# 64 experts: gating a unit ahead of weighing, slot rows eight units ahead, matrices reloaded at the second product

## The chip, the cores and the metric

The kernel runs on one core of a Trainium2 chip. The metric is the time of one execution on the device in microseconds (us), lower is better. A core has engines with their own instruction queues: TensorE (PE, its weight loads PEld), VectorE (DVE), ScalarE (ACT), GpSimd (POOL) and SyncE (SP, which here only issues DMA transfers). They wait for each other through semaphores: an instruction raises one when it is done, another queue waits for a count.

## The reference

The program is a stack of four macaron layers on 4096 tokens of width 128, each with two half-weighted feed-forward parts around an attention part. The first layer's feed-forward, used twice, is the mixture with 64 experts. Cut to what matters:

```python
def _L0_ffn_ref(hidden_states, wg, shared_w1, shared_w2, expert_w1, expert_w2):
    gates = jax.nn.softmax(logits, axis=-1)
    w_topk, idx_topk = jax.lax.top_k(gates, TOPK)          # 8 of 64
    ...
    valid = rank < CAPACITY                                # 160 slots an expert
    buf = jnp.zeros((NUM_EXPERTS, CAPACITY, H), x.dtype).at[se, rank].set(x[st], mode='drop')
    h = jnp.einsum('ech,efh->ecf', buf, expert_w1)         # 128 -> 2 x 384
    x1, x2 = jnp.split(h, 2, axis=-1)
    out = jnp.einsum('ecf,ehf->ech', x1 * jax.nn.silu(x2), expert_w2)   # 384 -> 128
    y = out[se, jnp.clip(rank, 0, CAPACITY - 1)]
    y = jnp.where(valid[:, None], y * sw[:, None].astype(y.dtype), 0.0)
    combined = jnp.zeros((T, H), x.dtype).at[st].add(y)
    return (shared_out + combined).reshape(B, S, H)
```

## The kernel before

All is float32. The mixture is done in three steps. The routing computes gates and scatters each chosen token's normalized row into the slot rows, a table in HBM of 10240 slots (64 x 160); a slot's row holds the 128 values, 64 weights and the token's number. Then `experts` works through the slots. Then `combine` adds two tables of results to the tokens.

`experts` takes 64 units, one expert each, a unit being 160 slots as 2 blocks (A = 2) of 80. For unit n, in the names of the profile (`l0f1e_` in the first run, `l0f2e_` in the second):

- SP loads the slot rows into `row` and the expert's matrices into `m_w` (393 KB and 197 KB). `Matrices` has four places; the first four experts' are loaded during the routing.
- TensorE turns the rows (`turn`, L3040, into bank `x`), ScalarE copies them to `xeT` (`copy`, L3081).
- TensorE makes the first product (`hidden`, L3050, bank `h`), six matrices, shown as twelve in the profile.
- ScalarE takes the silu of one half (`bend`, L3087, `sT`), VectorE multiplies it with the other (the gating, L3109, `gT`).
- TensorE makes the second product (`output`, L3060, bank `o`).
- VectorE reads the token numbers (L3117, `idx`) and multiplies the result with the slot's weight (the weighing, L3119, `y`).
- GpSimd scatters `y` with addition into one of two tables, one indirect DMA for each of the two blocks (L3153); unit n goes to table n % 2.

The order is written out by hand, one loop for each engine. TensorE's step n is `hidden(n + 1)`, `turn(n + 2)`, `output(n)`. ScalarE's is `bend(n)`, `copy(n + 2)`. VectorE's is gating n, index n, weighing n. Buffers: `row` 4, matrices 4, `y` and `idx` 4 (a ring), all others 2. The waits between them: VectorE may write `idx` and `y` of unit n when both scatters of unit n - 4 have landed; GpSimd starts the scatters of unit n when those of unit n - 2, into the same table, have landed; SP waits for the weighing of unit n - 4 (`y_ready`) and then issues matrices and slot rows of unit n in this order.

In the first run VectorE has work of another layer beside this: `kernel.products`, one instruction behind each weighing, 31 of 128x1024 elements and then a few small ones (L1841 in the profile, tiles `l0f1e_big`); it reads two SBUF operands. All 64 units are written out on VectorE there. In the second run it has none, and VectorE runs `stream`: the first steps written out, then a loop, then the last steps. The other engines do so in both runs, with four units a round.

## Time and profile before

| | us |
|---|---|
| median of 3 runs | 3244.47 (3237.09 to 3246.55) |
| the profiled execution | 3241.42 |
| its span | 3239.7 |
| GpSimd busy in the span | 1782.6 (55%) |
| TensorE busy | 2516.1 (78%) |
| VectorE busy | 2043.3 (63%) |
| mean granted TensorE clock | 0.893 |

All rows below are of that one profiled execution. A duration in the timeline is that of one instruction, or of so many merged (x12); what stands in brackets is the time that its engine stood idle before it and what ended that. A wait is put down to whatever came last by the profile; "issue" means that nothing the profile shows ended it. Idle time of an engine that isn't the bottleneck costs nothing. The expert step of the first run lies near 207 to 457 us, that of the second near 761 to 998 us.

### The profile page before, as it was taken

The page shows a single profiled execution, that of the slowest core. Times are in us where ns is not written, and L with a number is a line of the kernel's source. Part 1 is how long each engine was busy: PE and PEld are TensorE (multiplying, and loading weights), DVE is VectorE, ACT ScalarE, POOL GpSimd, SP SyncE. Part 2 cuts the span into 40 slices and gives each one's busy share as a digit, 9 for nine tenths or more (in the row PEclk, how much of TensorE's full clock was granted, in tenths as well). Part 3 has the DMA queues.
Part 4 walks back from the last instruction along what each step waited for, and adds up shares of the span by engine and source line. Part 5 has one row for each costly group of instructions (what it writes and reads, how often), then busy time and mean ns, then how long its engine had stood idle before and what let it go on. Part 6 is the DMA issues. An engine that isn't in the chain of part 4 may idle for free. (4 is left out here: it accounts for less than half of the span.)

```text
span 3239.7 us, 68607 instructions
## 1 busy us (share of the span) xinstructions
PE 2516.1 (78%) x24634; PEld 1640.8 (51%) x24634; DVE 2043.3 (63%) x5869; ACT 1372.1 (42%) x2937; POOL 1782.6 (55%) x2004
## 2 busy tenths in 40 slices
PE   3478957778994658899988999582898986999682
PEld 2358844547882434655555555370333333555371
DVE  6845335772334635588845887325999998788513
ACT  2212213321221324366652666334776762666433
POOL 4737752663874212399942134573888885123564
PEclk8689977879997879899987999795999998999796
DMA  9228862224996434001001011222121210111133
GB/s 374 94 67 206 220 163 50 89 64 105 233 224 185 117 111 191 19 17 21 13 2 22 20 28 36 69 72 99 73 103 55 82 76 14 20 26 33 47 96 96
DMA packets 220035, 294.11 MB, mean 91 GB/s; under 512 B 34016, under 2 KB 176895, under 8 KB 213600
## 3 DMA queue, kind: packets, MB, share of 16 engines
q1 hardware_dynamic: 173280, 249.85, 24.7%
q0 software_dynamic: 44352, 39.40, 6.4%
q8 instruction: 174, 2.85, 0.4%
q10 hardware_dynamic: 2112, 1.05, 0.2%
q14 instruction: 117, 0.96, 0.1%
HBM read 181.88 MB, written 100.40 MB: 87 GB/s over the span
## 5 line engine op out<-in xcount | busy, mean ns | idle before, releaser
L3873 POOL TENSOR_TENSOR l3am_db<-l3am_du,l3am_bs 128x1024 f32<-128x1024 f32 x127 | 297.8, 2367 | 38.4 <-DVE l3am_hh L4111 34.6
L4111 DVE TENSOR_TENSOR_SCAN l3am_hh<-l3am_dA,l3am_db 128x1024 f32<-128x1024 f32 x128 | 292.3, 2285 | 0.9 <-ACT l3am_dA L4011 0.7
L1217 POOL TENSOR_TENSOR l2a_pT<-l2a_pT,kept 128x512 int32<-128x512 int32 x213 | 265.0, 1281 | 45.4 <-ACT l2a_pT L1423 45.4
L4242 PE MATMUL l3am_y<-l3am_hc,ident 128*128 128x512 f32 x512 | 242.3, 596 | 0.0
L3153 POOL DMA_INDIRECT l0f_table<-l0f1e_y,l0f1e_idx x128 | 182.0, 1422 | 96.3 <-DVE l0f1e_y L3119 45.7
L3153 POOL DMA_INDIRECT l0f_table<-l0f2e_y,l0f2e_idx x128 | 178.8, 1397 | 98.2 <-DVE l0f2e_idx L3117 53.8
L4011 ACT ACTIVATE l3am_dA<-l3am_dl,l3am_al 128x512 f32<-128x512 f32 x256 | 166.3, 682 | 130.5 <-DVE l3am_hh L4111 126.9
L1304 DVE CUSTOM_DVE_ANT_0 l2a_junk<-l2a_s,addend 128x256 f32<-128x256 f32 x486 | 178.1, 421 | 56.8 <-PE l2a_s L1540 44.3
L1297 DVE TENSOR_REDUCE l3f1a_mx<-l3f1a_s 128x2 f32<-128x512 f32 x243 | 156.3, 684 | 40.2 <-PE l3f1a_s L1540 31.4
L1297 DVE TENSOR_REDUCE l3f2a_mx<-l3f2a_s 128x2 f32<-128x512 f32 x243 | 156.2, 684 | 36.1 <-PE l3f2a_s L1540 31.1
L1563 PE MATMUL l2a_e<-l2a_qk 32*128 32x256 f32 x964 | 161.1, 410 | 9.6 <-DVE l2a_pT L1225 8.8
L1423 ACT ACTIVATE l3f1a_pT<-l3f1a_e 128x512 f32<-128x512 f32 x241 | 133.1, 596 | 79.5 <-PE l3f1a_e L1563 75.8
L1423 ACT ACTIVATE l3f2a_pT<-l3f2a_e 128x512 f32<-128x512 f32 x241 | 133.1, 596 | 78.7 <-PE l3f2a_e L1563 75.7
L1540 PE MATMUL l3f1a_s<-l3f1a_qk 32*128 32x256 f32 x972 | 159.0, 421 | 3.5 <-DMA l3f1a_qk<-l3f1a_none 2.6
L4119 DVE TENSOR_TENSOR l3am_hc<-l3am_hh,l3am_c 128x1024 f32<-128x1024 f32 x128 | 153.7, 1200 | 7.2 <-PE l3am_c L4235 7.2
L1540 PE MATMUL l3f2a_s<-l3f2a_qk 32*128 32x256 f32 x972 | 154.7, 412 | 1.7 <-DVE l3f2a_mx L1297 1.7
L1563 PE MATMUL l3f1a_e<-l3f1a_qk 32*128 32x256 f32 x964 | 152.6, 411 | 0.1
L1563 PE MATMUL l3f2a_e<-l3f2a_qk 32*128 32x256 f32 x964 | 152.1, 410 | 0.1
L1540 PE MATMUL l2a_s<-l2a_qk 32*128 32x256 f32 x972 | 148.1, 410 | 0.0
L1939 POOL DMA_INDIRECT l0f_rows<-l0f1r_row,l0f1r_idx x110 | 112.3, 1021 | 55.4 <-issue 33.2
L4242 PEld LDWEIGHTS l3am_y<-l3am_hc,ident 128*128 128x128 f32 x512 | 98.4, 193 | 78.3 <-issue 74.5
L1423 ACT ACTIVATE l2a_pT<-l2a_e 128x512 f32<-128x512 f32 x203 | 114.8, 593 | 47.6 <-PE l2a_e L1563 45.6
(855 smaller groups left out, 6890.5 us busy)
## 6 DMA issues: line engine op xcount, KB each, us to landing
l3am_bs<-l3a_b SPq DMA_DIRECT2D x32, 1024.0 KB, 6.6
l0f1m_w<-in_L_ffn_expert_w SPq DMA_DIRECT2D x64, 384.0 KB, 3.2
l0f2m_w<-in_L_ffn_expert_w SPq DMA_DIRECT2D x64, 384.0 KB, 3.2
l1a_top<-l1a_kernel SPq DMA_DIRECT2D x16, 1024.0 KB, 11.8
l0f_rows<-blank SPq DMA_DIRECT2D x8, 1930.0 KB, 22.2
l0f1m_w<-in_L_ffn_expert_w SPq DMA_DIRECT2D x64, 192.0 KB, 3.3
l0f2m_w<-in_L_ffn_expert_w SPq DMA_DIRECT2D x64, 192.0 KB, 3.5
l3f_rows<-blank SPq DMA_DIRECT2D x8, 1440.0 KB, 12.1
```

The lines of the kernel that those rows point to most:

```text
L1217: self.nc.gpsimd.tensor_tensor(t, t, self.kept[:, f // 8 % 2, :].unsqueeze(1).to_broadcast([P, 2, 2 * P]), ALU.mult).then_inc(self.cut_g, 1)
L1297: self.nc.vector.tensor_reduce(self.mx[n % 3][:, t, col:col + 2], self.score_bank(f)[:, :].rearrange("p (h s) -> p h s", h=2), AX_X, ALU.m ...
L1304: m = self.nc.vector.tensor_tensor_reduce(out=self.junk[:, 2 * (f % 2) + q, :], in0=self.score_bank(f)[:, 2 * P * q:2 * P * q + 2 * P], in ...
L1423: self.nc.scalar.activation(self.pT[f % self.NP][:, :], self.prob_bank(f)[:, :], ACT.Exp).then_inc(self.p_ready, 1)
L1540: m = self.nc.tensor.matmul(self.score_bank(f)[:, 2 * P * q:2 * P * q + 2 * P], self.qk[n % 4][rows, s, 0, t * P:(t + 1) * P], self.qk[n % ...
L1563: m = self.nc.tensor.matmul(self.prob_bank(f)[:, 2 * P * q:2 * P * q + 2 * P], self.qk[b % 4][rows, s, 1, kh * P:(kh + 1) * P], self.qk[b ...
L3153: g.indirect_dma_start(out=tables[p], out_offset=bass.IndirectOffsetOnAxis(ap=idx[u % RING][:, a:a + 1], axis=0), in_=y[u % RING][:, a, :] ...
L3873: G.tensor_tensor(db[n % DB][:, :].rearrange("p (j t) -> p j t", j=CC), du[k % 2][:, :, :], bs[s // QUARTER][:, s % QUARTER, :].unsqueeze( ...
L4011: A.activation(dA[n % 2][:, halves[j]], dl[j][k % 2][:, :], ACT.Exp, scale=al[:, j, s:s + 1]).then_inc(dA_ready, 1)
L4111: V.tensor_tensor_scan(hh[n % HH][:, :], dA[n % 2][:, :], db[n % DB][:, :], 0.0, ALU.mult, ALU.add).then_inc(h_ready, 1)
L4119: V.tensor_tensor(hc[n % 2][:, :].rearrange("p (j t) -> p j t", j=CC), hh[n % HH][:, :].rearrange("p (j t) -> p j t", j=CC), cbk[:, :].uns ...
L4242: T.matmul(yb[j][:, :], c.ident[:, :], hc[n % 2][:, halves[j]], start=(s == 0), stop=(s == N - 1)).then_inc(summed, 1)
```

## The change

`moe64` and `attention_moe64` call a new function, `gated_experts`, in place of `experts`; `experts` stays for the mixtures with 8 experts. The instructions, their shapes and their number are the same. What differs:

- VectorE gates unit 0 first; its step n is then gating n + 1, index n, weighing n.
- ScalarE's step n is `bend(n + 1)`, `copy(n + 2)`, ahead of it `copy(0)`, `bend(0)`, `copy(1)`.
- `row` has 8 buffers in place of 4; the rows of unit n + 8 are loaded when unit n is weighed (`y_ready`).
- The matrices of unit n + 4 are loaded when the second product of unit n is made (`o_done`), no longer when it is weighed.
- The loops have eight units a round in place of four.

```diff
--- before.py
+++ after.py
+def gated_experts(nc, c, name, w, m, mats, E, C1, KC, A, kernel=None):
+    rows, tables, sub, V, PLACES, RING = m.rows, m.tables, SUB, 8, mats.places, 4
...
+        row = [ph.sb(f"row{i}", [sub, A, R]) for i in range(V)]
...
+            def step(at):
+                i, u, n = at(0)
+                if at(PLACES):
+                    sp.wait_ge(o_done, n + 1)
+                    mats.load(sp, at(PLACES)[2], u % PLACES)
+                if at(V):
+                    sp.wait_ge(y_ready, n + 1)
+                    load_rows(at(V)[2], u)
+
+            for u in range(V):
+                load_rows(u, u)
+            stream(sp, units, V, step)
...
+        def _(a_):
...
+            def step(at):
+                if at(1):
+                    bend(*at(1))
+                if at(2):
+                    copy(*at(2))
+
+            copy(0, 0, 0)
+            bend(0, 0, 0)
+            copy(0, 1, 1)
+            stream(a_, units, V, step)
...
+        def _(v):
...
+            def step(at):
+                i, u, n = at(0)
+                p = u % 2
+                if at(1):
+                    gate(*at(1))
+                if not isinstance(n, int) or n >= RING:
+                    v.wait_ge(added[p], 16 * A * ((V // 2) * i + (u - RING) // 2 + 1))
+                v.wait_ge(loaded[u % V], 16 * (i + u // V + 1))
+                nc.vector.tensor_copy(idx[u % RING][:, :], row[u % V][:, :, R - 1]).then_inc(idx_ready, 1)
+                v.wait_ge(o_done, n + 1)
+                nc.vector.tensor_tensor(y[u % RING][:, :, :], ob[p][0:sub, 0:A * D].rearrange("p (a d) -> p a d", a=A),
+                                        row[u % V][:, :, bass.ds(D + n, 1)].to_broadcast([sub, A, D]),
+                                        ALU.mult).then_inc(y_ready, 1)
+
+            gate(0, 0, 0)
...
-        experts(nc, c, name + "e", w, m, mats, 64, 6, 3, 2, True, kernel=kernel)
+        gated_experts(nc, c, name + "e", w, m, mats, 64, 6, 3, 2, kernel)
...
-        experts(nc, c, name + "e", w, m, mats, 64, 6, 3, 2, True)
+        gated_experts(nc, c, name + "e", w, m, mats, 64, 6, 3, 2)
```

VectorE at the beginning of the first run, before (`gT` is the gating, `idx` the token numbers, `y` the weighing, `big` a product of the other layer):

```order
L3109 TENSOR_TENSOR l0f1e_gT<-l0f1e_h,l0f1e_sT 128x480
L3117 CAST l0f1e_idx<-l0f1e_row 80x2
L3119 TENSOR_TENSOR l0f1e_y<-l0f1e_o,l0f1e_row 80x256
L1841 TENSOR_TENSOR l0f1e_big<-l0f1m_pr,l0f1m_cs 128x1024
L3109 TENSOR_TENSOR l0f1e_gT<-l0f1e_h,l0f1e_sT 128x480
L3117 CAST l0f1e_idx<-l0f1e_row 80x2
L3119 TENSOR_TENSOR l0f1e_y<-l0f1e_o,l0f1e_row 80x256
L1841 TENSOR_TENSOR l0f1e_big<-l0f1m_pi,l0f1m_sn 128x1024
```
And with the change:

```order
L3285 TENSOR_TENSOR l0f1e_gT<-l0f1e_h,l0f1e_sT 128x480 x2
L3295 CAST l0f1e_idx<-l0f1e_row 80x2
L3297 TENSOR_TENSOR l0f1e_y<-l0f1e_o,l0f1e_row 80x256
L1841 TENSOR_TENSOR l0f1e_big<-l0f1m_pr,l0f1m_cs 128x1024
L3285 TENSOR_TENSOR l0f1e_gT<-l0f1e_h,l0f1e_sT 128x480
L3295 CAST l0f1e_idx<-l0f1e_row 80x2
L3297 TENSOR_TENSOR l0f1e_y<-l0f1e_o,l0f1e_row 80x256
L1841 TENSOR_TENSOR l0f1e_big<-l0f1m_pi,l0f1m_sn 128x1024
```
A gating has moved from behind each product to ahead of the weighing before it; behind a product stands still a gating, but that of a unit later.

SP at the same place, before (names as above; what a row waits for stands in brackets):

```order
L3015 DMA l0f1e_row<-l0f_rows 80x2x193 x4
L3020 UNCONDITIONAL_BRANCH
L3020 ISA
L2954 ISA [waits l0f1e_y_ready]
L2954 DMA l0f1m_w_0<-in_L_ffn_expert_w 128x768
L2956 ISA
L2956 DMA l0f1m_w_0<-in_L_ffn_expert_w 128x384
L3015 ISA
L3015 DMA l0f1e_row<-l0f_rows 80x2x193
```
And with the change:

```order
L3198 DMA l0f1e_row<-l0f_rows 80x2x193 x8
L2954 DMA l0f1m_w_0<-in_L_ffn_expert_w 128x768 [waits l0f1e_o_done]
L2956 DMA l0f1m_w_0<-in_L_ffn_expert_w 128x384
L3198 DMA l0f1e_row<-l0f_rows 80x2x193 [waits l0f1e_y_ready]
L2954 DMA l0f1m_w_1<-in_L_ffn_expert_w 128x768 [waits l0f1e_o_done]
L2956 DMA l0f1m_w_1<-in_L_ffn_expert_w 128x384
L3198 DMA l0f1e_row<-l0f_rows 80x2x193 [waits l0f1e_y_ready]
L2954 DMA l0f1m_w_2<-in_L_ffn_expert_w 128x768 [waits l0f1e_o_done]
```
Eight row loads stand ahead of the first reload instead of four, each matrix load has a wait of its own on the second product, and each row load has one on the weighing.

## Rows read from the trace of the kernel before

**Rows 1.** The page's costliest groups: busy, mean ns, idle before.
```profile
L3153 POOL DMA_INDIRECT l0f_table<-l0f1e_y,l0f1e_idx x128 | 182.0, 1422 | 96.3 <-DVE l0f1e_y L3119 45.7
L3153 POOL DMA_INDIRECT l0f_table<-l0f2e_y,l0f2e_idx x128 | 178.8, 1397 | 98.2 <-DVE l0f2e_idx L3117 53.8
```

**Rows 2.** Busy us by stretch: PE, PEld, DVE, ACT, POOL; then PEclk, DMA share, GB/s.
```profile
219.00:344.00 125.00, 106.39 (x835) 100.61 (x834) 75.13 (x133) 25.26 (x64) 92.36 (x64) 1.00 0.82 204
...
773.00:998.00 225.00, 202.59 (x1613) 190.31 (x1612) 68.97 (x187) 48.68 (x123) 178.60 (x128) 1.00 0.86 214
```

**Rows 3.** Waits, 219 to 456 us: total, times, longest.
```profile
DVE l0f1e_y L3119 <- PE l0f1e_o L3060: 120.2, 63, 2.8
...
PE l0f1e_o L3060 <- DVE l0f1e_gT L3109: 19.0, 32, 1.1
```

**Rows 4.** Waits, 773 to 997 us.
```profile
PEld l0f2e_x L3040 <- DMA l0f2e_row<-l0f_rows: 25.7, 47, 2.0
...
POOL l0f_table L3153 <- DMA l0f_table<-l0f2e_y,l0f2e_idx: 4.7, 6, 1.2
```

**Rows 5.** Timeline, first run: start, duration, idle before in brackets.
```profile
299.80 0.42 DVE L3119 TENSOR_TENSOR l0f1e_y<-l0f1e_o,l0f1e_row 80x256 f32<-80x256 f32 x1 [1.50 <-PE l0f1e_o L3060]
...
300.14 1.21 DVE L1841 TENSOR_TENSOR l0f1e_big<-l0f1m_pr,l0f1m_cs 128x1024 f32<-128x1024 f32 x1
...
301.11 1.51 POOL L3153 DMA_INDIRECT l0f_table<-l0f1e_y,l0f1e_idx  x1 [0.66 <-issue]
...
301.38 0.66 DVE L3109 TENSOR_TENSOR l0f1e_gT<-l0f1e_h,l0f1e_sT 128x480 f32<-128x480 f32 x1
...
301.96 0.21 DVE L3117 CAST l0f1e_idx<-l0f1e_row 80x2 uint32<-80x2 f32 x1
...
302.09 1.54 PE L3060 MATMUL l0f1e_o<-l0f1m_w,l0f1e_gT 128*80 128x128 f32 x12 [0.56 <-DVE l0f1e_gT L3109]
...
303.67 0.42 DVE L3119 TENSOR_TENSOR l0f1e_y<-l0f1e_o,l0f1e_row 80x256 f32<-80x256 f32 x1 [1.50 <-PE l0f1e_o L3060]
```

**Rows 6.** Timeline, GpSimd, first run.
```profile
219.29 1.61 POOL L3153 DMA_INDIRECT l0f_table<-l0f1e_y,l0f1e_idx  x1 [40.81 <-DVE l0f1e_y L3119]
...
344.36 1.40 POOL L3153 DMA_INDIRECT l0f_table<-l0f1e_y,l0f1e_idx  x1 [1.22 <-DVE l0f1e_y L3119]
...
455.43 1.40 POOL L3153 DMA_INDIRECT l0f_table<-l0f1e_y,l0f1e_idx  x1 [0.30 <-issue]
```

**Rows 7.** Timeline, GpSimd, second run.
```profile
773.07 1.47 POOL L3153 DMA_INDIRECT l0f_table<-l0f2e_y,l0f2e_idx  x1 [51.87 <-DVE l0f2e_idx L3117]
...
787.97 1.39 POOL L3153 DMA_INDIRECT l0f_table<-l0f2e_y,l0f2e_idx  x1 [1.16 <-DMA l0f_table<-l0f2e_y,l0f2e_idx]
...
803.10 1.39 POOL L3153 DMA_INDIRECT l0f_table<-l0f2e_y,l0f2e_idx  x1 [1.46 <-DVE l0f2e_y L3119]
...
938.80 1.40 POOL L3153 DMA_INDIRECT l0f_table<-l0f2e_y,l0f2e_idx  x1 [1.62 <-DVE l0f2e_idx L3117]
...
996.83 1.40 POOL L3153 DMA_INDIRECT l0f_table<-l0f2e_y,l0f2e_idx  x1 [0.30 <-issue]
```

**Rows 8.** Timeline, VectorE's weighings, second run.
```profile
801.70 0.42 DVE L3119 TENSOR_TENSOR l0f2e_y<-l0f2e_o,l0f2e_row 80x256 f32<-80x256 f32 x1 [4.07 <-PE l0f2e_o L3060]
...
804.78 0.42 DVE L3119 TENSOR_TENSOR l0f2e_y<-l0f2e_o,l0f2e_row 80x256 f32<-80x256 f32 x1 [2.03 <-PE l0f2e_o L3060]
```

**Rows 9.** Timeline, routing ahead of the first run.
```profile
111.74 1.22 DVE L1774 SCALAR_TENSOR_TENSOR l0f1r_argi<-l0f1r_turns,l0f1r_argi 128x1024 f32<-128x1024 f32 x1
...
112.31 1.50 POOL L1939 DMA_INDIRECT l0f_rows<-l0f1r_row,l0f1r_idx  x1 [0.30 <-issue]
...
114.12 0.98 POOL L1939 DMA_INDIRECT l0f_rows<-l0f1r_row,l0f1r_idx  x1 [0.30 <-issue]
...
116.19 2.47 DVE L1774 SCALAR_TENSOR_TENSOR l0f1r_argi<-l0f1r_turns,l0f1r_argi 128x1024 f32<-128x1024 f32 x2
...
116.69 1.57 POOL L1939 DMA_INDIRECT l0f_rows<-l0f1r_row,l0f1r_idx  x1 [0.30 <-issue]
```

106 lines of the change are left out of this document (added).

## The prediction

> **What bounds the kernel now.** I read the page's costliest groups first, then the two expert stretches by themselves (busy time by stretch, waits), then single instructions in order of time. The change touches only the 64-expert layer, which runs twice. The scatters of its results into the tables, 128 by GpSimd in each run, are among the five costliest groups of the page [rows 1]. The first run lasts from its first scatter at 219.29 us to the end of the last at 455.43 + 1.40 = 456.83, the second from 773.07 to 996.83 + 1.40 = 998.23 [rows 6, 7]: 237.5 and 225.2 us for 64 units of work each. Everything below is about what paces these 463 us; the rest of the span has the same instructions as before.
>
> The reader should see three regimes.
>
> Units 0 to 31 of the first run (219.29 to 344.36 [rows 6], 125.1 us, 3.91 each) carry a 1.21 us product of another layer on VectorE, one behind each weighing. Here the pace is a loop through VectorE and TensorE: weighing starts at 299.80, product 0.34 later, gating 1.24 after that, the second product's matmuls 0.71 later, the next weighing 1.58 after those: 0.34 + 1.24 + 0.71 + 1.58 = 3.87 [rows 5]. VectorE waits 120 us of this run for the second product's output although it has work lined up, and TensorE waits 19 us for the gating [rows 3]. GpSimd is not the limit: it has two scatters per unit.
>
> Units 32 to 63 of the first run (344.36 to 456.83, 112.5 us, 3.51 each) have no product beside them. A scatter takes 1.40 and the next starts 0.30 later [rows 7], so two take 3.40: a floor of 108.8 us for 32 units. GpSimd is within 3.7 us of it.
>
> The second run has no products at all. GpSimd's busy time of 178.6 [rows 2] plus 127 gaps of 0.30 is 216.7 of its 225.2 us, so all that could be late here costs 8.5 us. TensorE waits 25.7 us for slot rows [rows 4], but most of that wait is off the path.
>
> So the engine that bounds two of the three regimes is not touched, and in the third it stands only 0.5 us per unit behind the loop.
>
> **The change part by part.** *Gating ahead of weighing.* In step n VectorE now gates unit n + 1, then weighs n, then does the product. The product leaves the loop. What is left of TensorE's own pace shows where nothing held it: weighings at 801.70 and 804.78 [rows 8], 3.08 per unit. VectorE's own sum is 0.58 (gating to index copy, 301.38 to 301.96 in time, less than its 0.66) + about 0.2 + 0.34 + 1.24 = 2.4, so it hides under 3.08. Next in line is GpSimd at 3.40. If that were all, units 0 to 31 would fall from 3.91 to the 3.51 of the other half: 12.8 us.
>
> It is not all. A scatter that starts while a product runs is held. The scatter at 301.11 took 1.51 instead of 1.40 and ended at 302.62; the product ended at 301.35 [rows 5]. Take off 1.40 and its real start was 301.22, 0.13 before the product's end. In the routing the same arithmetic holds with a whole half microsecond: the two-input operation from 111.74 ends at 112.96, the scatter from 112.31 ends at 113.81, where the one from 114.12, with nothing in its way, takes 0.98; so it began at 112.83, again 0.13 before that end; the one from 116.69 was held 0.59 [rows 9]. Yet the second operation of that pair, which began some 0.15 after the scatter had got going, neither waited (two in 2.47) nor held it [rows 9]. So a product closes a window of 1.21 - 0.13 = 1.08 us to scatter starts. Today the loop puts the product right behind the weighing that the next scatter waits for, and that scatter starts 1.31 after the weighing starts, when the window is nearly over: loss 0.11 [rows 5]. Once GpSimd is behind with its work, its starts fall anywhere in the window.
>
> Cost: starts come every 1.70, so a product catches one with chance 1.08 / 1.70 = 0.64 and then holds it 0.54 on average: 0.34 per unit, 3.40 + 0.34 = 3.74. The phase is not random at first. While VectorE is free of the ring of four y buffers the product comes every 3.08, two of them in 6.16, and three scatters from one release take 1.08 + 3 x 1.70 = 6.18: the fourth start falls 0.02 inside a window, is held again, and the pattern repeats with three scatters in 6.16, 4.11 per unit. If it falls just ahead of the window instead, five go in three products, 3.70. For the first nine units, until the ring is full (GpSimd loses 0.3 to 1.0 per unit; a weighing may not pass the landing four units back), I take the middle, 3.9; for the other 23, 3.74: 35.1 + 86.0 = 121.1, against 125.1. **Term A: -4.0**, with bounds from no hold at all (3.51: -12.8) to one full hold per unit (3.40 + 1.08 = 4.48: +18.3).
>
> *Units 32 to 63.* At 344.36 GpSimd had waited 1.22 for a weighing, 0.9 above the usual gap [rows 6]; with GpSimd behind this goes. Its other late starts are waits for landings or nothing shown. **Term B: -0.9**, bounds 0 and the whole excess, -3.7.
>
> *Slot rows eight ahead, matrices at the second product.* Both remove reasons for TensorE to be late. In the second run GpSimd was late on their account at 803.10 (1.46, behind a weighing that a row load held up) and at 938.80 (1.62, index copy) [rows 7]: 1.16 + 1.32 = 2.5. The wait for a landing of the table two units back (787.97, 1.16 [rows 7]; 4.7 us in all [rows 4]) stays: nothing here makes the landing earlier. **Term C: -2.5**, bounds -8.5 (all excess gone) and +6, because the transfers are nearly the third limit: the share of 0.86 over 225 us is 3.0 us of all DMA engines per unit and 0.82 over 125 us is 3.2 [rows 2]; at 3.7 per unit the latter becomes 0.86, and landings like that of 787.97 may become common. +6 is 0.1 per unit.
>
> *Costs at the start.* ScalarE now bends unit 0 before it copies unit 1, so TensorE gets that operand later, about one copy's place, 0.2 us; VectorE gates unit 1 ahead of weighing 0, which was due 0.6 later anyhow. SP issues eight row loads instead of four ahead of the first matrix reload, which isn't due until the first output. In steady state the bend comes ahead of the copy of the following unit; the copy must be ready when the 1.5 us of the second product are over, and 0.57 + 0.30 fits. SP's order per unit is two matrix loads, then a row load that waits for the weighing; behind that wait stand the next unit's matrices, which aren't needed for two units. **Term D: +0.4** for both runs (0 to 1).
>
> Sum: -4.0 - 0.9 - 2.5 + 0.4 = -7.0. The profiled execution took 3241.4 us (span 3239.7), so 3234.4 on its footing; the median shown is 3.1 above it, which would make 3237.5. I predict 3236.
>
> **The rivals.** *The products don't hold the scatters at other phases.* Every accumulating scatter seen here met only the last 0.1 to 0.2 of a product; only plain scatters were held long [rows 5, 9]. Then units 0 to 31 run at 3.51: -12.8 in place of -4.0, total -15.8, about 3227. Against it: both kinds are held to the same 0.13. The Trainium skill (SBUF — State Buffer, Who interferes with whom) would have it so: it infers that a tensor_tensor takes only the read side of the shared port pair and does not stall descriptor generation. By that rule the sum is this rival's; the held starts in this trace disagree with it. Chance 0.13.
>
> *The product becomes GpSimd's brake, and the kernel is slower.* When the ring of y is full, VectorE's weighing, and the product behind it, start a fixed time after a landing, which itself is a fixed time after a scatter: the phase can lock where each product catches a start nearly in full. It decides from the point at which units 0 to 31 take over 3.91 + 3.0/32 = 4.0 each; at the 4.11 of the resonance it costs 32 x 0.2 = +6.4 in place of -4.0, total +3.4; a loss over 9.7 us needs 4.3; at 4.48 it is +18.3 - 3.0, about 3260. For it: three in 6.18 against 6.16 is nearly exact. Against it: landings scatter by tenths, which breaks a phase. Chance 0.15.
>
> *Landings become the limit.* TensorE ahead of GpSimd brings the matrices in bursts; if the last 96 units take 0.08 more each, that is +7.7 against B and C, and the sum is near zero: 3243. Against it: ring and places bound how far TensorE can be ahead. Chance 0.17.
>
> **How the numbers follow.** Forecast 0.55, with its own range 3229 to 3242. A measurement of this kernel tells apart about 0.3%, 9.7 us, so faster means under 3234.7. Of the forecast I give 0.4 to that side, 0.6 to the same; first rival all faster; second half slower, half same; third same. Faster 0.22 + 0.13 = 0.35, same 0.33 + 0.08 + 0.17 = 0.57 (rounded), slower 0.08. Range 3223 to 3249: the bottom takes in most of the first rival with runs below the median, the top the landings and the resonance.
>
> **What would show it.** Right: TensorE's waits for gating and slot rows gone; GpSimd back to back through both runs; units 0 to 31 at 3.65 to 3.85 with scatters of 1.5 to 2.4 us among those of 1.40, each ending 1.27 after a product's end, so that the mean of the first run's scatters rises from 1422 [rows 1] to about 1500; the second run at 222 to 223 us. Wrong: no scatter above 1.6 (first rival); units 0 to 31 at 4.0 or more (second); more than 4.7 us of GpSimd's waits put down to landings and a second run of 225 or more (third).

## The result, and the profile after

The changed kernel takes 3281.03 us (median of 4 runs, 3273.27 to 3284.77), the kernel before 3245.51 beside it (4 runs): ratio 1.0107, 95% interval 1.0085 to 1.0129. It is slower by about 1% (the whole interval lies above 1), and its median lies above the range of the prediction, 3223 to 3249. Its profiled execution took 3273.27 us, its span is 3271.6, 31.9 longer than before.

The groups of the page that answer to [rows 1] (busy, mean ns, idle before):

```profile
L3325 POOL DMA_INDIRECT l0f_table<-l0f1e_y,l0f1e_idx x128 | 200.0, 1563 | 96.5 <-DVE l0f1e_y L3297 40.1
...
L3325 POOL DMA_INDIRECT l0f_table<-l0f2e_y,l0f2e_idx x128 | 178.9, 1398 | 113.1 <-DVE l0f2e_y L3297 54.3
```

GpSimd's timeline gives the three regimes, as [rows 6, 7] do for before:

```profile
217.54 1.61 POOL L3325 DMA_INDIRECT l0f_table<-l0f1e_y,l0f1e_idx  x1 [39.50 <-DVE l0f1e_y L3297]
...
354.00 1.40 POOL L3325 DMA_INDIRECT l0f_table<-l0f1e_y,l0f1e_idx  x1 [1.69 <-DMA l0f_table<-l0f1e_y,l0f1e_idx]
...
473.18 1.40 POOL L3325 DMA_INDIRECT l0f_table<-l0f1e_y,l0f1e_idx  x1 [0.30 <-issue]
...
795.13 1.47 POOL L3325 DMA_INDIRECT l0f_table<-l0f2e_y,l0f2e_idx  x1 [53.13 <-DVE l0f2e_y L3297]
...
1032.64 1.40 POOL L3325 DMA_INDIRECT l0f_table<-l0f2e_y,l0f2e_idx  x1 [0.30 <-issue]
```

The busy time by stretch, columns as in [rows 2] (the fifth is GpSimd; then clock, DMA share, GB/s):

```profile
217.50:354.00 136.50, 118.42 (x915) 115.96 (x913) 74.17 (x138) 27.57 (x72) 110.28 (x64) 0.95 0.81 201
354.00:474.60 120.60, 86.82 (x698) 83.71 (x698) 29.21 (x86) 19.71 (x51) 89.74 (x64) 0.95 0.71 168
795.00:1034.00 239.00, 197.79 (x1614) 192.74 (x1612) 69.46 (x188) 47.28 (x123) 178.88 (x128) 0.97 0.80 199
```

| us | before | after | difference |
|---|---|---|---|
| first run, units 0 to 31 | 125.1 | 136.5 | +11.4 |
| first run, units 32 to 63 | 112.5 | 120.6 | +8.1 |
| second run | 225.2 | 238.9 | +13.7 |
| all the rest of the span | 2776.9 | 2775.6 | -1.3 |

All three got longer. There are two kinds of loss, scatters that take longer and gaps between scatters, and GpSimd's column tells them apart. 64 scatters of 1.40 are 89.6 us of work. In units 32 to 63 it is busy for 89.74 and in the second run for 178.88: nothing in the scatters, everything in the gaps between them. In units 0 to 31 it is busy for 110.28, where before had 92.36 [rows 2]: 20.7 us of scatters that were held, in place of 2.8. The floor of 32 units is 108.8 us, so of the 27.7 us over it in units 0 to 31 the other 7.0 are gaps.

*The gaps.* Waits of the changed kernel, 795 to 1034 us (total, times, longest); before, VectorE had no wait of the first kind in the second run, and GpSimd's, the second, came to 4.7 us [rows 4]:

```profile
DVE l0f2e_idx L3295 <- DMA l0f_table<-l0f2e_y,l0f2e_idx: 130.3, 39, 5.9
...
POOL l0f_table L3325 <- DMA l0f_table<-l0f2e_y,l0f2e_idx: 25.5, 21, 1.8
```

And those of the SP queue in the same stretch:

```profile
SPq L3198 <- DVE l0f2e_y L3297: 87.8, 24, 5.1
SPq L2954 <- PE l0f2e_o L3242: 28.4, 18, 3.9
```

VectorE now waits for landings of scatters four units back: TensorE and VectorE have run ahead until the ring of four `y` was full. What follows from that is seen in the timeline (TensorE's second products, VectorE, SP's queue, GpSimd):

```profile
926.42 1.47 PE L3242 MATMUL l0f2e_o<-l0f2m_w,l0f2e_gT 128*80 128x128 f32 x12
...
930.12 0.17 DVE L3295 CAST l0f2e_idx<-l0f2e_row 80x2 uint32<-80x2 f32 x1 [5.72 <-DMA l0f_table<-l0f2e_y,l0f2e_idx]
...
930.24 0.42 DVE L3297 TENSOR_TENSOR l0f2e_y<-l0f2e_o,l0f2e_row 80x256 f32<-80x256 f32 x1
...
930.89 1.40 POOL L3325 DMA_INDIRECT l0f_table<-l0f2e_y,l0f2e_idx  x1 [1.51 <-DMA l0f_table<-l0f2e_y,l0f2e_idx]
...
931.22 0.41 DVE L3297 TENSOR_TENSOR l0f2e_y<-l0f2e_o,l0f2e_row 80x256 f32<-80x256 f32 x1
...
931.36 1.53 PE L3242 MATMUL l0f2e_o<-l0f2m_w,l0f2e_gT 128*80 128x128 f32 x12 [1.62 <-DVE l0f2e_gT L3285]
...
931.37 0.33 SPq L2954 DMA_DIRECT2D l0f2m_w<-in_L_ffn_expert_w  x1
...
933.30 0.33 SPq L2954 DMA_DIRECT2D l0f2m_w<-in_L_ffn_expert_w  x1
...
937.68 0.17 DVE L3295 CAST l0f2e_idx<-l0f2e_row 80x2 uint32<-80x2 f32 x1 [5.46 <-DMA l0f_table<-l0f2e_y,l0f2e_idx]
...
938.34 1.40 POOL L3325 DMA_INDIRECT l0f_table<-l0f2e_y,l0f2e_idx  x1 [0.95 <-DMA l0f_table<-l0f2e_y,l0f2e_idx]
...
939.09 0.34 SPq L2954 DMA_DIRECT2D l0f2m_w<-in_L_ffn_expert_w  x1
...
940.75 0.33 SPq L2954 DMA_DIRECT2D l0f2m_w<-in_L_ffn_expert_w  x1
```

Weighings come in pairs: 930.24 and 931.22, 0.98 apart, then none until 937.89. Both second products had long been made (the later of the two ended at 926.42 + 1.47 = 927.89), so when the landing comes the second weighing needs only its own landing and the gating between. SP stood at a row load that waits for the weighing, with one unit's matrices behind it; these leave at 931.37. The next unit's leave at 933.30, when the second product that the first gating had released (931.36 + 1.53 = 932.89) is done. So two units' matrices (1.2 MB) leave within 2.5 us, and the next pair only at 939.09 and 940.75. GpSimd waits 1.51 and 0.95 us for landings here, and these late landings release the next pair. That the landings are late because they share the DMA engines with the burst is inferred: the profile gives no time from issue to landing for these scatters. The experiments below take the bursts away.

### The profile page after: what moved, and what is told of

Read it like the earlier page. It is cut to its first block and busy times, and to the rows that moved or that the text cites. A ratio compares the mean times of both kernels' runs of the same rounds, so it can differ in the third digit from the quotient of the medians.

```text
span 3271.6 us, 68101 instructions
## 1 busy us (share of the span) xinstructions
PE 2510.9 (77%) x24634; PEld 1652.4 (51%) x24634; DVE 2038.7 (62%) x5869; ACT 1370.4 (42%) x2937; POOL 1802.5 (55%) x2004
## 5 line engine op out<-in xcount | busy, mean ns | idle before, releaser
L3325 POOL DMA_INDIRECT l0f_table<-l0f1e_y,l0f1e_idx x128 | 200.0, 1563 | 96.5 <-DVE l0f1e_y L3297 40.1
## 6 DMA issues: line engine op xcount, KB each, us to landing
l1a_top<-l1a_kernel SPq DMA_DIRECT2D x16, 1024.0 KB, 12.9
l3f_rows<-blank SPq DMA_DIRECT2D x8, 1440.0 KB, 11.2
```

Source lines behind the costliest of these rows:

```text
L3325: g.indirect_dma_start(out=tables[p], out_offset=bass.IndirectOffsetOnAxis(ap=idx[u % RING][:, a:a + 1], axis=0), in_=y[u % RING][:, a, :] ...
```

## Experiments

Times of the three regimes in each kernel's profile, worked out as above, and the ratio of the timed kernels to before on the same chip (e1 to e4 ran on one chip, later groups on others):

| kernel | units 0-31 | 32-63 | second run | ratio (95%) |
|---|---|---|---|---|
| before | 125.1 | 112.5 | 225.2 | 1 |
| after | 136.5 | 120.6 | 238.9 | 1.0107 [1.0085, 1.0129] |
| e1 gating ahead only | 114.8 | 110.6 | 228.0 | 0.9981 [0.9964, 0.9999] |
| e2 loads only | 124.7 | 113.6 | 228.0 | 1.0002 [0.9986, 1.0018] |
| e3 after, no reloads | 143.4 | 109.1 | 217.7 | one run |
| e4 before, no reloads | 125.0 | 109.0 | 217.6 | one run |
| e5 after, rows two units later | 128.8 | 114.0 | 226.4 | 1.0016 [0.9996, 1.0036] |
| e6 after, matrices at the weighing | 135.0 | 125.5 | 248.7 | 1.0157 [1.0119, 1.0194] |
| e7 e1 + matrices at the product | 123.7 | 112.2 | 223.8 | 1.0015 [0.9997, 1.0032] |
| e8 gating ahead, first run only | 125.7 | 111.4 | 226.3 | 0.9973 [0.9955, 0.9991] |
| e9 e8, products in quarters | 131.6 | 115.1 | 223.5 | 1.0032 [1.0019, 1.0045] |
| e10 after, in quarters | 143.8 | 121.1 | 239.2 | one run |
| e11 after, products behind | 120.8 | 127.4 | 240.0 | one run |
| e12 e5, in quarters | 129.8 | 114.1 | 226.6 | 1.0037 [1.0015, 1.0058] |
| e13 e3, products behind | 109.3 | 115.1 | 217.6 | one run |
| e14 e3, products 0.4 later | 115.3 | 109.2 | 218.2 | one run |
| e15 e8, product at the announcement | 117.2 | 112.1 | 227.1 | one run |
| e16 e15, 0.4 later | 137.0 | 110.0 | 224.7 | 0.9998 [0.9980, 1.0017] |
| e17 e8, VectorE in step | 121.6 | 109.5 | 226.5 | 0.9977 [0.9960, 0.9994] |
| e18 after, VectorE in step | 125.9 | 114.1 | 227.7 | 1.0003 [0.9990, 1.0016] |

The regimes are those of one execution, the profiled one, the ratios those of all runs. The profiled execution of e8 took 10.7 us more than the median of its runs (3242.81 against 3232.09), that of e16 7.0 more, those of e7 and e12 8.5 and 12.3 less. So a difference of some 10 us in a regime between two kernels isn't shown by one profile of each; 28 us are.

**Which half of the change costs the time.** e1 is before with this part of the diff alone, rows four ahead and all loads as before (shortened; unit 0 is bent and gated ahead of the loop):

```diff
 ScalarE      def step(at):
-                bend(*at(0))
+                if at(1):
+                    bend(*at(1))
...
 VectorE      def step(at):
...
-                gate(*at(0))
+                if at(1):
+                    gate(*at(1))
```

> Only the gating and the bend one unit ahead; slot rows four ahead and matrices with them, as before. Theory 1 (the slot rows four ahead were a brake: a row that is asked for when unit n is weighed is there some 4.7 us later and the second product of n + 2 stands behind it, 6.7 us for two units, 3.35 a unit, so TensorE hardly gained on GpSimd's 3.40; eight ahead lift the brake, VectorE fills the ring of y, and units then pass in pairs): second run 225 +- 2 us as before, units 32 to 63 of the first 111 to 114, units 0 to 31 118 to 125 (loop gone, products hold some scatters), whole kernel 3232 to 3247. Theory 2 (the order of VectorE and ScalarE is what breaks the pace, whatever the loads): second run 235 or more, whole kernel 3265 or more.

e2 is after with those lines turned back, so rows eight ahead and matrices at `o_done`.

> Only the loads changed: slot rows eight ahead, matrices when the second product is made, eight units a round; VectorE and ScalarE in the old order. Theory 1: units 0 to 31 of the first run 125 us as before (the loop through product and gating holds the pace), then the pairs appear: units 32 to 63 near 118 to 121, second run 236 to 240, whole kernel 3258 to 3270. Theory 2: all three parts as before, 3245 +- 8.

Neither half costs what the whole does: e1 is even slightly faster than before (its interval ends at 0.9999), e2 the same. In e2 VectorE waits 126.4 us of the second run for landings, as long as in after, so the ring is full there too, and yet the run takes 228.0 and not 238.9; what I had expected from a full ring was wrong. Its weighings stay at least 2.6 us apart there, where those of after come down to 0.97: with the gating behind the weighing, the next second product, and so the next weighing, waits for it. The second-run weighings of all the kernels say the same. Only after, e6, e10 and e11, the four with gating ahead, rows eight ahead and the matrices behind a wait for a weighing, and nothing else that slows VectorE down (as e18 has), have neighbours less than 1.5 us apart (14, 21, 17 and 15 times), and only these four have a second run over 230 us. It takes both parts.

**Is it the transfers?** e3 and e4 are after and before with the matrices loaded once, so that from the fifth unit on the wrong experts' matrices are used, in products of the same shape (the lines are those of e3):

```diff
-                if at(PLACES):
-                    sp.wait_ge(o_done, n + 1)
-                    mats.load(sp, at(PLACES)[2], u % PLACES)
...
-                pe.wait_ge(mats.loaded[u % PLACES], mats.LOADED * matrices_use(i, u))
+                pe.wait_ge(mats.loaded[u % PLACES], mats.LOADED)
```

> The changed kernel without reloading the matrices (the first four experts' matrices are used for all 64). If the lost time is scatters that land late behind matrix transfers, these landings come back under 3.7 us and GpSimd is back to back: second run 217 to 219 us, units 32 to 63 of the first 109; units 0 to 31 keep only the holds by the products, 112 to 131. If it is something in the order itself (ring waits, TensorE's bursts), the second run stays over 230.

> The kernel before without reloading the matrices (the first four experts' are used for all). Units 0 to 31 of the first run should stay at 125 us under both theories, since the loop paces them; units 32 to 63 at 109 to 110 and the second run at 217 to 219, the floor of 1.70 a scatter. Beside the changed kernel without reloads it tells what the order alone does.

Without matrix loads both kernels run units 32 to 63 in 109 and the second run in 218 us: the floor of 3.40 per unit (108.8 and 217.6). So all of the loss there, 11.8 and 21.3 us over the floor, comes with the matrix loads. TensorE hardly waits for them (0.3 us, once, in the second run of after), and e3 has no pairs in its second run although gating and rows are ahead. What changes is how long other transfers take: a row load of the second run lands 3.4 us after its issue in after (median), 2.1 in e3. TensorE's clock isn't the reason. In units 32 to 63 it was granted 0.95 in after, and in e3 too, which ran at the floor (columns as above):

```profile
362.00:471.00 109.00, 87.44 (x693) 83.41 (x691) 29.44 (x85) 19.77 (x52) 89.58 (x64) 0.95 0.41 50
```

Units 0 to 31 went the other way: 143.4 in e3, over the 112 to 131 that I had expected, against 125.0 in e4. A second mechanism sits there, taken up below.

**Which load makes the pairs.** e5 is after with the row load later, for unit n + 6 when unit n - 2 is weighed; e6 is after with matrices at `y_ready` again; e7 is e1 with matrices at `o_done`.

```diff
e5
-                if at(V):
-                    sp.wait_ge(y_ready, n + 1)
-                    load_rows(at(V)[2], u)
+                if at(V - 2) and (not isinstance(n, int) or n >= 2):
+                    sp.wait_ge(y_ready, n - 1)
+                    load_rows(at(V - 2)[2], (u - 2) % V)
e6
-                    sp.wait_ge(o_done, n + 1)
+                    sp.wait_ge(y_ready, n + 1)
e7
+                    if not stay:
+                        sp.wait_ge(o_done, n - U + 1)
+                        mats.load(sp, n, p)
                     sp.wait_ge(y_ready, n - U + 1)
-                    if not stay:
-                        mats.load(sp, n, p)
```

> The changed kernel, but a slot row is loaded two weighings later: after unit n - 2 is weighed, for unit n + 6, so that SP does not stand at a row load with the next unit's matrices behind it. Theory 1 (the pairs come from SP's queue: it waits for a weighing that the full ring holds back, and two units' matrices then go out together): the matrix loads go out 3 to 4.5 us apart, not 6.4 and 1.6; second run 225 to 231 us, units 32 to 63 of the first 112 to 115; units 0 to 31 stay at 132 to 140, since the products still hold the scatters. Theory 2 (the pairs come from VectorE's ring wait alone): second run 236 to 240 as in the changed kernel, whole kernel within 5 us of 3281.

> The changed kernel with the matrices loaded when unit n is weighed, as before, the rows eight ahead and the gating ahead. Theory 1 (what breaks the pace is rows eight ahead together with the gating ahead): as slow as the changed kernel, 3270 to 3290, since matrices that wait for the weighing come in pairs as well. Theory 2 (loading the matrices at the second product is the culprit): near the kernel with the gating alone, 3230 to 3245.

> The gating ahead with slot rows four ahead, the matrices loaded when the second product is made. Theory 1: the rows four ahead keep the brake, so it stays with the gating alone, 3228 to 3240. Theory 2: close to the changed kernel, over 3260.

e5 takes the wait for the weighing out of the matrices' way, and 12.5 us of the 13.7 in the second run are gone, the pairs with them (units 0 to 31, at 128.8, came out below the 132 to 140 that I had expected). e6 ties the matrices to the weighings altogether, and it is no better than after (248.7 in the second run; ratio 1.0157, whose interval just overlaps that of after). e7 has the matrices at the second product without rows eight ahead: no loss against before, though at 3242.92 it missed my 3228 to 3240. Loading the matrices at `o_done` makes no pairs; what hurts is a load queue that stands behind a weighing. The pairs and the bursts keep each other up: without the bursts (e3, e5) there are no pairs either.

e8 is e1 with the gating ahead in the first run only (`ahead_ = gated and kernel is not None`). It has the lowest ratio of the timed kernels, within what I had expected, though those of e1 and e17 lie inside its interval.

> The gating ahead in the first run alone, the second run and all loads as before. The first run then takes 225 us as with the gating alone (before 237), the second 225 to 226 (228 with the gating alone, 225 before, which may be noise): whole kernel 3227 to 3236, ratio to before 0.995 to 0.998. If the 12 us are no real gain of the loop's removal, it comes out within 3 us of before.

**The held scatters.** e11 moves all 31 products behind unit 63 (the line `next(products, None)` goes from the loop):

> The changed kernel with all products of the other layer behind the 64 units instead of one behind each. Units 0 to 31 of the first run in 116 to 122 us, no scatter held (mean 1400 to 1410 ns), since the pairs alone are left; units 32 to 63 118 to 122. The first run as a whole ends some 30 us later for the products behind it, so the kernel's time says nothing on the change.

Units 0 to 31 fall from 136.5 to 120.8, the pace that the others have in after. (Units 32 to 63, 127.4, are longer than expected: the moved products stand beside its last scatters.) e13 does the same to e3:

> After with two things taken out: the matrices are loaded once and not again (units from the fifth on use the wrong experts' matrices; the work is the same), and the 31 products stand behind the 64 units instead of one behind each weighing. With the matrices gone and the products kept, units 0 to 31 took 143.4 us, the others 109.1 and the second run 217.7. Theory 1 (the products alone hold the scatters there): units 0 to 31 fall to the floor of two scatters per unit, 32 x 3.40 = 109, mean scatter of the first run 1.40, second run 217 to 218 as without the change here. Theory 2 (something else in the gating ahead also slows the first half, such as the first units' landings): 115 us or more.

Units 0 to 31 fall from 143.4 to 109.3, the floor. So with the transfers gone the products alone cost 34 us, 1.1 for each (units 32 to 63 are longer because the moved products stand beside its last scatters: GpSimd is busy for 95.6 us there, not 89.6). How is seen in e3's timeline:

```profile
299.37 2.60 POOL L3322 DMA_INDIRECT l0f_table<-l0f1e_y,l0f1e_idx  x1 [0.30 <-DMA l0f_table<-l0f1e_y,l0f1e_idx]
299.48 1.21 DVE L1841 TENSOR_TENSOR l0f1e_big<-l0f1e_big 128x1024 f32<-128x1024 f32 x1
...
302.27 1.40 POOL L3322 DMA_INDIRECT l0f_table<-l0f1e_y,l0f1e_idx  x1 [0.31 <-issue]
303.63 0.17 DVE L3292 CAST l0f1e_idx<-l0f1e_row 80x2 uint32<-80x2 f32 x1 [2.25 <-DMA l0f_table<-l0f1e_y,l0f1e_idx]
303.71 0.41 DVE L3294 TENSOR_TENSOR l0f1e_y<-l0f1e_o,l0f1e_row 80x256 f32<-80x256 f32 x1
303.98 2.56 POOL L3322 DMA_INDIRECT l0f_table<-l0f1e_y,l0f1e_idx  x1 [0.30 <-issue]
304.04 1.21 DVE L1841 TENSOR_TENSOR l0f1e_big<-l0f1m_pr,l0f1m_cs 128x1024 f32<-128x1024 f32 x1
```

The scatter at 299.37 starts 0.11 us *before* the product at 299.48 and is held all the same: 299.37 + 2.60 - 1.40 = 300.57, 0.12 before the product's end. And the phase is locked: landing, index, weighing, product follow at fixed distances, so nearly every product meets a scatter's first tenths (30 of the 31 hold one, for 1.13 us on average).

My first remedy was to cut the products into four of 128x256 (in e8, after and e5):

```diff
-            link(V.tensor_tensor(o, a, b, op))
+            pieces = o.shape[1] if o.shape[1] == 4 else 1
+            for j in range(pieces):
+                s = slice(j, j + 1) if pieces == 4 else slice(None)
+                done[0] += 1
+                V.tensor_tensor(o[:, s], a[:, s], b[:, s], op).then_inc(self.summed, 1)
+            v.wait_ge(self.summed, done[0])
```

> The gating ahead in the first run alone, and each product of the other layer in four pieces of 128x256. Theory 1 (a scatter is held only if it starts inside a two-input operation, to 0.13 us before its end): a piece of some 0.35 us closes 0.2 us, so the four together catch a start with chance 0.5 for 0.1 us, 0.05 us a unit instead of 0.34 and more: units 0 to 31 in 110 to 114 us, mean scatter of the first run under 1420 ns, whole kernel 3218 to 3230, clearly under the version with whole products (3232). Theory 2 (what counts is how long VectorE reads two operands in all, whatever the pieces): units 0 to 31 stay at 118 to 126, whole kernel 3230 to 3240.

> The changed kernel with each product in four pieces. Theory 1 (two losses add up: held starts, and pairs of units with late landings): units 0 to 31 of the first run fall from 136 to 117 to 122 us, the pace of its other half with its pairs; units 32 to 63 (120) and the second run (239) stay. Theory 2 (the pairs follow from the held starts): the pairs go in the first run, units 32 to 63 under 115.

> The changed kernel with both losses taken away: slot rows loaded two weighings later, for unit n + 6 (SP no longer waits at them), and products in four pieces. Theory 1: units 0 to 31 in 111 to 115 us, units 32 to 63 112 to 115, second run 225 to 228, whole kernel 3226 to 3236. If a third loss is left in the order, it stays at 3240 or more.

It failed in all three: units 0 to 31 got no shorter (125.7 and 131.6 in e8 and e9, 136.5 and 143.8 in after and e10, 128.8 and 129.8 in e5 and e12), and e9's ratio, 1.0032, lies clear above e8's 0.9973. The timeline of e9 (x4 is four pieces in a row):

```profile
266.00 2.78 POOL L3172 DMA_INDIRECT l0f_table<-l0f1e_y,l0f1e_idx  x1 [0.31 <-DVE l0f1e_idx L3134]
266.09 1.42 DVE L1845 TENSOR_TENSOR l0f1e_big<-l0f1m_pi,l0f1m_sn 128x256 f32<-128x256 f32 x4
```

Four pieces behind each other hold a scatter to the end of the last (266.00 + 2.78 - 1.40 = 267.38, they end at 267.51), and last 1.42 instead of 1.21.

I then laid the starts of products and scatters beside each other in the first runs of the 15 profiles with whole products. Where a product started from 1.0 us before to 0.25 behind a scatter's start, 291 of 296 scatters were held by more than 0.1 us; from 0.25 to 0.375 behind, 15 of 53; later still, while the scatter ran, none of 260. Four of the five exceptions are in e15; one of them, where both start together and it is the product that takes a little longer (1.26 for 1.22):

```profile
284.37 1.26 DVE L1841 TENSOR_TENSOR l0f1e_big<-l0f1m_pr,l0f1m_cs 128x1024 f32<-128x1024 f32 x1 [0.49 <-POOLq L3170]
284.37 1.40 POOL L3172 DMA_INDIRECT l0f_table<-l0f1e_y,l0f1e_idx  x1 [0.30 <-DMA l0f_table<-l0f1e_y,l0f1e_idx]
```

The gatings and weighings, which have one of their two inputs in PSUM, hold nothing: in no second run of the 20 profiles did a scatter take more than 1.47 us. e14 tests the rule: e3 with each product put off by four tiny copies.

```diff
                     step(lambda d: (0, n + d, n + d) if n + d < units else None)
+                    if n < 31:
+                        v.wait_ge(y_ready, n + 1)
+                        v.wait_ge(spared, 4 * n)
+                        for j in range(4):
+                            nc.vector.tensor_copy(spare[:, j, :], y[n % RING][:, :, 0]).then_inc(spared, 1)
                     next(products, None)
...
```

> After with the matrices loaded once only (units from the fifth on use the wrong experts' matrices), the products in their place, but each put off by four copies of 80x2 elements ahead of it, about 0.35 to 0.4 us. The traces so far say: a scatter is held to 0.13 us before the product's end if the product starts anywhere from 1.1 us before to 0.3 us after the scatter's start, and not at all if it starts later than that. Without the delay the products started 0.1 us before to 0.3 us after a scatter, all held, units 0 to 31 took 143.4 us. Theory 1 (the product locks to the scatter through the landing, and only its phase decides): now they start 0.3 to 0.7 us after one and end before the next starts, so units 0 to 31 take 109 to 118 us although each unit has more work; mean scatter of the first run under 1.48. Theory 2 (the phase locks where the hold is, whatever the offset): 135 us or more, mean scatter 1.6 or more.

```profile
302.67 1.40 POOL L3329 DMA_INDIRECT l0f_table<-l0f1e_y,l0f1e_idx  x1 [0.30 <-issue]
302.70 0.38 DVE L3309 CAST l0f1e_spare<-l0f1e_y 80x2 uint32<-80x2 f32 x4
302.99 1.21 DVE L1841 TENSOR_TENSOR l0f1e_big<-l0f1e_big 128x1024 f32<-128x1024 f32 x1
...
304.38 1.40 POOL L3329 DMA_INDIRECT l0f_table<-l0f1e_y,l0f1e_idx  x1 [0.30 <-issue]
```

The product now starts 0.32 behind the scatter and holds neither this one nor the next. VectorE has more to do, and units 0 to 31 take 115.3 instead of 143.4 us; the one run of the whole kernel is 32 us shorter than that of e3 (3214.87 against 3247.11, on another chip). Seven scatters are still held, and they make up 5.3 of the 6.1 us that GpSimd is busy over 89.6. So it is the phase that decides, and not how much VectorE has to do.

**Setting the phase on purpose.** In e15 and e16 GpSimd raises `going` ahead of its scatters, and VectorE waits for it ahead of each product of e8; e16 puts four copies between.

```diff
 GpSimd
+                if kernel:
+                    g.sem_inc(going, 1)
                 for a in range(A):
 VectorE
+                    if n < 31:
+                        v.wait_ge(going, n + 1)
                     next(products, None)
```

> The version with gating ahead in the first run alone (slot rows four ahead), and VectorE waits before each product until GpSimd has announced the two scatters of that unit: GpSimd raises a semaphore right ahead of the first of them. If the announcement comes just ahead of the scatter's start, the product starts 0 to 0.2 us behind that start, inside the 0.3 us in which it still holds it: theory 1: each unit 3.40 + about 1.2 = 4.6 us, units 0 to 31 140 to 148 us, mean scatter of the first run 1.65 to 1.70. Theory 2 (a scatter is only held by a product that began before it): 109 to 112 us. Theory 3 (the announcement comes early, while the scatter before still runs): something between, with the offset to be read in the trace.

> As the kernel in which VectorE waits for GpSimd's announcement ahead of each product, but with four copies of 80x2 elements (0.35 to 0.4 us) between the wait and the product. Theory 1 (only a product that starts from 1.1 us before to 0.3 us after a scatter's start holds it): the product starts about 0.4 us behind the first scatter of its unit and ends 0.1 us before the second, nothing is held: units 0 to 31 take 109 to 112 us, mean scatter of the first run 1.40 to 1.42, about 3225 to 3232 in all against 3232 with gating ahead in the first run alone. Theory 2 (it is held whatever the distance, by the share of time that VectorE reads two operands): 120 us or more and no faster than before.

The third theory of e15 held: the announcement comes early, while the scatter before still runs. The product that it releases starts 0.71 us or more ahead of the scatter behind the announcement, in the middle of the 31 cases 0.95; the 0.85 of the expectations below is nearer the low end.

```profile
302.01 1.40 POOL L3172 DMA_INDIRECT l0f_table<-l0f1e_y,l0f1e_idx  x1 [0.30 <-issue]
...
302.81 1.22 DVE L1841 TENSOR_TENSOR l0f1e_big<-l0f1e_big 128x1024 f32<-128x1024 f32 x1 [1.28 <-POOLq L3170]
...
303.72 1.58 POOL L3172 DMA_INDIRECT l0f_table<-l0f1e_y,l0f1e_idx  x1 [0.31 <-issue]
```

The product starts 0.80 behind one scatter and 0.91 ahead of the next, which is held 0.18. e16's delay then shifted it into the next scatter's start, and units 0 to 31 took 137.0, with 23.5 us of held scatters against 6.4 in e15: my expectation for e16 missed for that reason, and its distance from e15 fits the phase again. e17 and e18 move the wait ahead of the gating, so that gating, index, weighing and the four copies, which stay ahead of each product, are the delay. e17 does it in e8, in the first run alone; e18 does it to the unchanged loads and order of after, in all units of both runs (the lines are those of e18; the copies and `going` are left out):

```diff
                 if at(1):
+                    if not isinstance(n, int) or n >= 1:
+                        v.wait_ge(going, n)
                     gate(*at(1))
```

> The version with gating ahead in the first run alone (slot rows four ahead); in units 1 to 32 of the first run VectorE waits, ahead of the gating of the next unit, until GpSimd has announced the scatters of the unit before, and four copies of 80x2 elements stand ahead of each product. The traces of the two paced kernels show the announcement 0.85 us ahead of the scatter's start; gating 0.58, index 0.07, weighing 0.46 and the copies 0.28 bring the product to 0.5 to 0.6 us behind that start, behind the 0.3 in which it is still held, and its end to about the next start. The weighing comes 3 us ahead of its own scatter. Theory 1 (only the phase decides): units 0 to 31 take 109 to 113 us against 125.7 and 137.0 in the profiles of the version without pacing and of the wrongly placed one, mean scatter of the first run 1.40 to 1.43, ratio to before 0.991 to 0.995. Theory 2 (holds come whatever the phase, or the pacing costs as much): 118 us or more, ratio 0.997 or more.

> After itself, with its gating ahead, its rows eight ahead and its matrix loads at the second product all kept, but VectorE waits in all units of both runs, ahead of the gating of the next unit, until GpSimd has announced the scatters of the unit before; four copies of 80x2 elements stand ahead of each product of the first run. Theory 1 (the loss came from two things, VectorE running ahead until weighings come in pairs and SP's loads in bursts, and products at the wrong phase): weighings come one by one every 3.4 to 3.5 us, units 0 to 31 fall from 136.5 to 109 to 114, units 32 to 63 from 120.6 to 110 to 114, the second run from 238.9 to 219 to 227; ratio to before 0.990 to 0.998. Theory 2 (rows eight ahead with matrices at the second product slow the transfers by themselves): second run 232 us or more, units 32 to 63 117 or more, ratio over 1.000.

e17 missed: 121.6, and a ratio of 0.9977 where I had expected 0.991 to 0.995, no better than e8. The product still starts anywhere from 0.4 behind to 1.3 ahead of a scatter's start; what moves it is not shown. e18 settles the pairs: its second run has none. Its waits in the second run, and its stretches (units 0 to 31, 32 to 63, second run):

```profile
DVE l0f2e_gT L3288 <- POOLq L3334: 143.6, 57, 3.9
...
POOL l0f_table L3336 <- DMA l0f_table<-l0f2e_y,l0f2e_idx: 5.0, 7, 1.6
```

```profile
218.19:344.07 125.88, 109.08 (x868) 105.55 (x867) 82.43 (x254) 26.01 (x68) 103.41 (x64) 0.99 0.87 210
344.07:458.17 114.10, 93.40 (x747) 89.71 (x745) 31.10 (x89) 21.23 (x55) 89.71 (x64) 0.97 0.82 187
775.54:1003.24 227.70, 200.98 (x1612) 193.90 (x1610) 66.47 (x188) 47.25 (x123) 178.84 (x128) 0.99 0.86 209
```

With gating ahead, rows eight ahead and matrices at the second product all kept, and VectorE made to *wait* 143.6 us, GpSimd's waits for landings are back from 25.5 to 5.0, and the three regimes lose 10.6, 6.5 and 11.2 us: 28 of the 33 that the change had added. The ratio, 1.0003, is that of no change, and not the 0.990 to 0.998 that I had expected. The second run missed the upper end of my expectation by 0.7, units 32 to 63 by 0.1, units 0 to 31 by 12: there the products still held scatters by 13.8 us (103.41 - 89.6).

## Why the prediction was wrong

The frame held: GpSimd bounds all three regimes after the change, the floor is 3.40 per unit (109 and 218 in e3 and e4), and the rest of the span hardly moved (-1.3). The signs of the terms did not. I had -7.0 for the span and it was +31.9: terms B and C were off by 9.0 and 16.2 us, term A by 15.4.

*Terms B and C (-0.9 and -2.5; measured +8.1 and +13.7).* The step that failed is the overlap that I took for free, in the sentence (under the costs at the start) that behind the row load's wait "stand the next unit's matrices, which aren't needed for two units". It is true of TensorE, which rarely waits for them. But I asked only who needs the matrices, not what else their transfers share the DMA engines with, nor when they leave. The third rival named this mechanism, bursts of matrices that delay landings, and priced it at 0.08 per unit; the measured price is (8.1 + 13.7) / 96 = 0.23. The bound of term C, +6, was too narrow for the same reason. The argument against the rival, that ring and places bound how far TensorE can be ahead, was the wrong one: it is exactly the full ring that lines two ready units up behind one landing. Its marks came as listed: 25.5 us of waits for landings against 4.7, second run over 225. e4 shows that the excess over the floor in the second run before, 7.6 us, comes with the matrix loads as well. The 2.5 of term C were read from two late starts; no kernel with rows eight ahead and matrices reloaded gained them (228.0 in e2, 226.4 in e5).

*Term A (-4.0; measured +11.4).* The loop did go: VectorE's waits for the second product, 120.2 us [rows 3], are gone. TensorE's for the gating are not: 35.3 us over the first run in place of 19.0, since a VectorE that stands at a landing gates late too; with the ring full that need not cost anything. The term that failed is the cost of the hold. I took the window of a product from its start to 0.13 before its end, 1.08 us; it opens about 0.3 us earlier, 1.38. By the prediction's own working that is a chance of 1.38 / 1.70 = 0.81 and 0.69 on average, 0.56 per unit and not 0.34: 17.9 us in 32 units. In after 27 of the 31 products held a scatter, and GpSimd's busy time gives 20.7 us, 0.65 per unit. The trace of before could not show the early edge, since every product beside its 64 units started about 1.0 us before a scatter or 1.1 behind one. The rest of the 27.7 us over the floor, 7.0, are gaps between scatters; the weighings come in pairs here too, 2.2 and some 6 us apart in turn, with the product between the two. In e18, without pairs, the holds are 13.8 and the gaps 3.3, so most of the 10.6 us between the two are shorter or fewer holds. In the other kernels with the loop gone and single weighings the holds are 4.7 us (e1), 11.1 (e17), 12.9 (e7), 13.1 (e8) and 17.8 (e5), and units 0 to 31 take 114.8 to 128.8. So a random phase is no fixed price: in e7, e8 and e5 the holds take back all or most of the 12.8 us that the loop cost, in e1 they don't. The second rival's mark, over 4.0 per unit, also came (136.5 / 32 = 4.27), and its lock at nearly a full hold is what e3 shows at 4.5; in after the lock doesn't last, and its price is near the random one.

The Trainium skill (SBUF — State Buffer, Who interferes with whom) infers that a tensor_tensor doesn't stall descriptor generation. For the scatters of this kernel the traces show otherwise: beside a TENSOR_TENSOR a scatter of e3 takes 2.60 us and not 1.40, and the same products and scatters at another phase (e14) make units 0 to 31 28 us shorter.

*Term D (+0.4).* The first scatter came at 217.54 against 219.29. It is too small to judge: the stretch between the two runs, whose code is the same, alone differs by 4 us (316.2 before, 320.6 after).

*The chances.* The second and third rival, 0.15 and 0.17, were treated as exclusive and each as small; they came together, and the mechanism that joins them is one I had in hand: an engine taken off its brake runs until a buffer is full, and from then on its work comes in step with a landing. I should have asked, for each of its instructions, what that step does.

What stays open: why e1 and e8, whose first runs have the same code, take 114.8 and 125.7 us in units 0 to 31. The products' phase differs in the two traces (4.7 and 13.1 us of holds), but what sets it in an execution without a lock was not found; executions of one and the same kernel differ by as much in all, so it may be no property of the kernel. No version with products at a chosen phase kept it through the run, so the 109 of the floor was reached only without products.

## What to carry to other kernels

An engine that waits often is a brake as well: before taking its wait away, find which buffer it will fill, and ask what will release its work then, one by one or in pairs. A queue of loads should not have a wait for late work ahead of loads whose timing matters, even if nobody needs those loads yet; here their bursts went with late landings of other work. Where two engines disturb each other only at certain moments, the phase counts more than the amount of work: 0.4 us more per unit made 28 us less (e14, without matrix loads), and pacing VectorE by GpSimd gave back 28 (e18).

## What the runs showed of the hardware

- A scatter of 80 rows is held by a VectorE operation of 1.21 us with two SBUF inputs, even if that starts up to about 0.3 us *behind* the scatter's own start (291 of 296 cases, 15 of 53 at the edge, none of 260 beyond); it goes on about 0.13 us before the operation's end. The longest hold by one product was 1.45 us (e6). The product itself is no longer for it (1.21 to 1.23); only two, of 1.26 and 1.27 in e15, were, and these started together with a scatter that wasn't held.
- Operations with one of two inputs in PSUM, of 0.66 and 0.42 us, hold no scatter: none of any second run took more than 1.47 us.
- Back to back, four such operations of 0.41 us hold like one of 1.42 (e9).
- A semaphore that GpSimd raises ahead of a scatter lets VectorE start 0.71 us or more, mostly about 0.95, before that scatter does (e15), while the scatter before still runs, so the semaphore is no mark of the start.
- Four copies of 80x2 on VectorE with their wait put the product off by 0.39 us: it starts 0.73 behind the weighing's start in e14, 0.34 in e3.
